# Queries ahead of attention and tokens ahead of keys in a one-core MetaFormer block

## The reference

```
n  = layernorm over channels(x)                        # eps 1e-6
k  = relu(Wk n + bk);  q = relu(Wq n + bq);  v = Wv n + bv     # 1x1 convolutions, 8 heads of 8 channels
context  = k v^T, summed over all 16384 pixels of an image, per head
x1 = x + Wr (context^T q) + br
t  = layernorm over channels(x1)                       # eps 1e-5
p  = softmax(t router_w + router_b)                    # 8 experts; the two largest kept, normalised to sum 1
out = x1 + sum over the two experts of p_e * (t expert_w[e] + expert_b[e])
```

## Time and profile before

| what | value |
|---|---|
| median of 3 runs | 696.85 us (696.65 to 698.34) |
| profiled execution, its own time | 696.26 us |
| its span, first to last instruction | 694.4 us |
| TensorE matmuls busy | 632.0 us (91%) |
| VectorE busy | 531.5 us (77%) |
| ScalarE busy | 422.6 us (61%) |
| GpSimd busy | 396.6 us (57%) |
| mean granted TensorE clock | 0.99 |

### The profile page before, as it was taken

One profiled execution on the slowest core, in us unless ns is written; L12 is line 12 of the kernel. 1 busy time (PEld: TensorE's weight loads), 2 busy tenths in 40 slices (PEclk: granted clock), 3 DMA queues, 4 the chain that ended last, 5 costly groups with the idle time before them and its releaser, 6 DMA issues.

```text
span 694.4 us, 21531 instructions
## 1 busy us (share of the span) xinstructions
PE 632.0 (91%) x8318; PEld 281.6 (41%) x8318; DVE 531.5 (77%) x1176; ACT 422.6 (61%) x832; POOL 396.6 (57%) x350
## 2 busy tenths in 40 slices
PE   3799899799999999999999999999988989896886
PEld 1566655444444444444444444443222223231222
DVE  3443457788788988887888888877999898988854
ACT  2355466767576776767576676767566575664542
POOL 7132432166556656656555665555766566575785
PEclk9999999999999999999999999999999999999999
DMA  6223545755566565555556655444655555463442
GB/s 144 61 66 94 124 123 135 177 135 138 122 154 153 125 151 140 126 133 139 120 141 154 147 129 123 107 119 114 150 123 122 122 123 136 102 149 85 106 107 47
DMA packets 32664, 86.22 MB, mean 124 GB/s; under 512 B 7651, under 2 KB 7827, under 8 KB 32563
## 3 DMA queue, kind: packets, MB, share of 16 engines
q1 hardware_dynamic: 32082, 84.64, 50.9%
q0 software_dynamic: 288, 0.19, 0.1%
q10 hardware_dynamic: 192, 0.01, 0.0%
HBM read 34.47 MB, written 16.78 MB: 74 GB/s over the span
## 4 chain that ended last, share of the span: by engine, by line
PE 62%; DVE 21%; issue 8%; ACT 7%; POOL 1%; DVEq 0%; ACTq 0%; POOLq 0%
PE bank L1077 24%; PE bank L1000 7%; PE bank L1063 7%; PE bank L978 5%; DVE z L812 4%; PE bank L947 4%; DVE x L716 3%; PE bank L1074 3%; DVE osb L822 2%; ACT grows L560 2%; PE bank L1049 2%; PE bank L964 2%; PE bank L923 2%; PE bank L909 2%; PE bank L1024 1%
## 5 line engine op out<-in xcount | busy, mean ns | idle before, releaser
L433 POOL TENSOR_TENSOR z<-gbs,x1d 128x512 f32<-128x512 f32 x256 | 320.8, 1275 | 212.3 <-ACT gbs L566 113.9
L1080 PE MATMUL bank<-z,ew 128*64 128x512 f32 x512 | 247.7, 607 | 0.0
L1077 PE MATMUL bank<-z,ew 128*64 128x512 f32 x512 | 247.6, 607 | 0.0
L812 DVE TENSOR_TENSOR z<-bank,x1d 128x512 f32<-128x512 f32 x256 | 163.2, 679 | 19.6 <-PE bank L1063 19.3
L566 ACT COPY gbs<-bank 128x512 f32<-128x512 f32 x256 | 140.4, 594 | 55.3 <-PE bank L1063 52.3
L1063 PE MATMUL bank<-grows,sel 64*64 64x512 f16 x1024 | 98.3, 391 | 27.9 <-DVE z L812 17.0
L424 POOL TENSOR_TENSOR xsq<-xin 128x512 f32<-128x512 f32 x64 | 65.4, 1044 | 78.3 <-DMA xin<-in_x_dram 74.4
L1077 PEld LDWEIGHTS bank<-z,ew 128*64 128x64 f32 x512 | 65.7, 138 | 105.6 <-issue 95.7
L494 ACT COPY xn<-bank 128x512 f32<-128x512 f32 x64 | 34.4, 589 | 77.0 <-PE bank L923 77.0
L671 DVE TENSOR_TENSOR xnT<-bank,rstd 128x512 f32<-128x512 f32 x64 | 41.2, 685 | 36.8 <-PE bank L909 34.6
L1063 PEld LDWEIGHTS bank<-grows,sel 64*64 64x64 f16 x1024 | 26.9, 104 | 103.4 <-issue 29.8
(11 more groups left out here) (135 smaller groups left out, 823.9 us busy)
## 6 DMA issues: line engine op xcount, KB each, us to landing
x1d<-x SPq DMA_DIRECT2D x128, 256.0 KB, 4.4
xin<-in_x_dram SPq DMA_DIRECT2D x64, 256.0 KB, 4.1
x_again<-in_x_dram SPq DMA_DIRECT2D x64, 256.0 KB, 4.1
out_dram<-osb SPq DMA_DIRECT2D x128, 128.0 KB, 2.4
k<-in_const_dram SPq DMA_DIRECT2D x1, 453.5 KB, 3.8
ew_nat<-in_L_ffn_expert_w_dram POOLq DMA_DIRECT2D x2, 64.0 KB, 6.3
sel<-in_const_sel_dram SPq DMA_DIRECT2D x1, 128.0 KB, 3.4
bk_rows<-bk_wide ACTq DMA_DIRECT2D x6, 1.0 KB, 1.7
```

The lines of the kernel that those rows point to most:

```text
L433: pool.tensor_tensor(z[:, 1, i % R_Z, :], gbs[:, i % R_Z, :], x1d[:, g % 2, 1, u * NT:(u + 1) * NT], ALU.mult).then_inc(z_pool, 1)
L812: dve.tensor_tensor(z[:, 0, i % R_Z, :], bank[:, :], x1d[:, g % 2, 0, u * NT:(u + 1) * NT], ALU.mult).then_inc(taken_of(("spread", i, 0)), 1)
L1077: pe.matmul(out_bank[0:C, :], ew[:, j, :], z[:, 0, i % R_Z, :], start=False, stop=(j == PAIRS - 1), skip_group_check=True).then_inc(prod_d ...
L1080: pe.matmul(out_bank[C:P, :], ew[:, j, :], z[:, 1, i % R_Z, :], start=False, stop=(j == PAIRS - 1), skip_group_check=True).then_inc(prod_d ...
```

## The change

In slot 2 TensorE and ScalarE take the queries first, then the first spread, then attention; before it was attention, first spread, queries. The bank list follows, and the ring of queries gets a ninth slot. In slot 0, from n = 17 on, TensorE transposes tokens first, then makes columns, then keys; ScalarE takes columns before keys. On VectorE `normalise` goes ahead of the gate steps of its slot, and the first z product of slot 2 ahead of the residuals. The work values of the deviation steps move from SBUF (`bstat`) to PSUM bank 7 (`dev_work`, in the columns of `g_all`), and 1 + exp goes to columns of `g_own` (`second_work`), for which `choose` moves behind the reciprocal. The 27 gate steps get other phases, `root_dev` moves from phase 0 to phase 1 (slot 2 of an even step), and the first gate step now waits for `low` of the pair before.

The parts below are, in order: the ring and the banks, ScalarE (slot 0, where TensorE's list changes likewise, and slot 2), the gate steps and slots of VectorE, and slot 2 of TensorE.

```diff
-R_X, R_Q, R_X1, R_Z = 3, 8, 7, 4
+R_X, R_Q, R_X1, R_Z = 3, 9, 7, 4
...
-        bstat = sb("bstat", [P, 5, QG])
-        gstat = sb("gstat", [P, 6, QG])
+        bstat = sb("bstat", [P, 4, QG])
+        gstat = sb("gstat", [P, 5, QG])
...
+        dev_work = [bank[7][:, QG * E + QG * i:QG * E + QG * (i + 1)] for i in range(2)]
+        second_work = bank[7][:, 0:QG]
...
-            gate_steps = {0: root_dev, 5: exponent, 7: high, 8: low}
+            gate_steps = {1: root_dev, 5: exponent, 7: high, 8: low}
...
-                    if k == 0:
+                    if k == 0 and n >= L_EXPERTS:
+                        if has_rows(n - L_COLS):
+                            take_cols(n - L_COLS)
+                        if real(n - L_KEYS):
+                            for s in range(S):
+                                take_keys(n - L_KEYS, s)
+                    elif k == 0:
...
-                        for i in iterations(n, k + 1)[:1]:
-                            copy_gates(i)
                         if real(n - L_KEYS):
                             for s in range(S):
                                 take_queries(n - L_KEYS, s)
+                        for i in iterations(n, k + 1)[:1]:
+                            copy_gates(i)
...
+                    upto(dve, low_done, p * 2)
-                    return dve.scalar_tensor_tensor(halves(bstat[:, 0, :]), mean, -1.0, mean, ALU.mult, ALU.mult)
+                    return dve.scalar_tensor_tensor(halves(dev_work[0]), mean, -1.0, mean, ALU.mult, ALU.mult)
...
-                dev = newton(bstat[:, 3, :], bstat[:, 4, :], bstat[:, 2, :], (bstat[:, 1, :], bstat[:, 0, :]))
+                dev = newton(bstat[:, 0, :], bstat[:, 3, :], bstat[:, 1, :], dev_work)
-                    lambda: dve.tensor_tensor(halves(bstat[:, 1, :]), halves(bstat[:, 0, :]), square, ALU.add),
-                    lambda: dve.tensor_scalar(bstat[:, 2, :], bstat[:, 1, :], 0.0, EPS_FFN, ALU.max, ALU.add),
-                    lambda: dve.reciprocal(bstat[:, 0, :], bstat[:, 2, :]),
+                    lambda: dve.tensor_tensor(halves(dev_work[1]), halves(dev_work[0]), square, ALU.add),
+                    lambda: dve.tensor_scalar(bstat[:, 1, :], dev_work[1], 0.0, EPS_FFN, ALU.max, ALU.add),
+                    lambda: dve.reciprocal(bstat[:, 2, :], bstat[:, 1, :]),
...
+                    lambda: dve.tensor_scalar(second_work, gstat[:, 4, :], 1.0, None, ALU.add),
+                    lambda: dve.reciprocal(gstat[:, 3, :], second_work),
                     choose,
-                    lambda: dve.tensor_scalar(gstat[:, 3, :], gstat[:, 5, :], 1.0, None, ALU.add),
-                    lambda: dve.reciprocal(gstat[:, 4, :], gstat[:, 3, :]),
                     gate,
...
-            gates_by_phase = {8: (26, 27), 0: (0, 4), 2: (4, 9), 3: (9, 12), 4: (12, 16), 6: (16, 20), 7: (20, 26)}
+            gates_by_phase = {8: (26, 27), 1: (0, 4), 2: (4, 10), 3: (10, 12), 4: (12, 14), 5: (14, 16), 6: (16, 23), 7: (23, 26)}
...
+                    if k == 0 and real(n - L_TURN):
+                        for s in range(S):
+                            normalise(n - L_TURN, s)
                     if k == 1:
...
                     if k == 2:
                         if real(n - L_EXPERTS):
                             result(n - L_EXPERTS, 0)
+                        for i in iterations(n, k + 1)[:1]:
+                            product(i)
                         if real(n - L_ATTEND):
...
+                        if real(n - L_KEYS):
+                            make_queries(n - L_KEYS)
+                        for i in iterations(n, k + 1)[:1]:
+                            broadcast(i)
                         if real(n - L_ATTEND):
                             attend(n - L_ATTEND)
-                        for i in iterations(n, k + 1)[:1]:
-                            broadcast(i)
-                        if real(n - L_KEYS):
-                            make_queries(n - L_KEYS)
```

More of the change, by code:

```diff
@@ L74, in bank_uses @@
                 yield "fold", *folding(n, k)
-            if k == 0:
+            if k == 0 and n >= L_EXPERTS:
+                if real(n - L_TURN):
+                    yield from (("turned", n - L_TURN, s) for s in range(S))
+                if has_rows(n - L_COLS):
+                    yield "cols", n - L_COLS, 0
+                if real(n - L_KEYS):
+                    yield from (("keys", n - L_KEYS, s) for s in range(S))
+            elif k == 0:
                 if real(n - L_KEYS):
@@ L87, in bank_uses @@
             if k == 2:
+                if real(n - L_KEYS):
+                    yield from (("queries", n - L_KEYS, s) for s in range(S))
+                for i in iterations(n, k + 1)[:1]:
+                    yield from (("spread", i, s) for s in range(S))
                 if real(n - L_ATTEND):
                     yield from (("attended", n - L_ATTEND, u) for u in range(U))
-                for i in iterations(n, k + 1)[:1]:
-                    yield from (("spread", i, s) for s in range(S))
-                if real(n - L_KEYS):
-                    yield from (("queries", n - L_KEYS, s) for s in range(S))
             if k == 3:
@@ L532, in root_dev @@
                 act.wait_ge(gate_dve, p * N_GATE + 4)
-                nc.scalar.activation(bstat[:, 4, :], bstat[:, 0, :], ACT.Sqrt).then_inc(dev_root, 1)
+                nc.scalar.activation(bstat[:, 3, :], bstat[:, 2, :], ACT.Sqrt).then_inc(dev_root, 1)
             def exponent(p):
@@ L538, in exponent @@
                 nc.scalar.activation(gex[:, :, :], g_own, ACT.Exp).then_inc(exp_done, 1)
-                nc.scalar.activation(gstat[:, 5, :], gstat[:, 2, :], ACT.Exp).then_inc(exp_done, 1)
+                nc.scalar.activation(gstat[:, 4, :], gstat[:, 2, :], ACT.Exp).then_inc(exp_done, 1)
             def high(p):
@@ L724, in gates @@
                 first = first_wins.unsqueeze(1).to_broadcast([P, QG, E])
-                over_dev = over_experts(bstat[:, 3, :])
+                over_dev = over_experts(bstat[:, 0, :])
                 def start():
@@ L736, in choose @@
                 def choose():
-                    dve.wait_ge(exp_done, p * 2 + 2)
                     return dve.tensor_tensor(g_own, g_all, gex[:, :, :], ALU.mult)
                 def gate():
-                    return dve.tensor_tensor(g_all, g_own, over_experts(gstat[:, 4, :]), ALU.mult)
+                    return dve.tensor_tensor(g_all, g_own, over_experts(gstat[:, 3, :]), ALU.mult)
                 def left():
@@ L748, in scale @@
                 def scale():
-                    upto(dve, low_done, p * 2)
                     return dve.tensor_tensor(by_half(g_own),
@@ L766, in less_second @@
                 def less_second():
[L767 removed]
+                    dve.wait_ge(exp_done, p * 2 + 2)
                     return less(g_all, 2)()
[L770 removed]
+                dev = newton(bstat[:, 0, :], bstat[:, 3, :], bstat[:, 1, :], dev_work)
                 steps = [
                     start,
[L773 to L775 removed]
+                    lambda: dve.tensor_tensor(halves(dev_work[1]), halves(dev_work[0]), square, ALU.add),
+                    lambda: dve.tensor_scalar(bstat[:, 1, :], dev_work[1], 0.0, EPS_FFN, ALU.max, ALU.add),
+                    lambda: dve.reciprocal(bstat[:, 2, :], bstat[:, 1, :]),
                     rooted, dev[1], dev[2],
@@ L890, in _ @@
                             gates(quad_in(n, k, phase), k0, k1)
-                    if k == 0 and real(n - L_TURN):
-                        for s in range(S):
-                            normalise(n - L_TURN, s)
-                    for i in iterations(n, k + 1):
+                    for i in iterations(n, k + 1)[1 if k == 2 else 0:]:
                         product(i)
@@ L1109, in _ @@
                         fold(*folding(n, k))
-                    if k == 0:
+                    if k == 0 and n >= L_EXPERTS:
+                        if real(n - L_TURN):
+                            turn_x(n - L_TURN)
+                        if has_rows(n - L_COLS):
+                            to_columns(n - L_COLS)
+                        if real(n - L_KEYS):
+                            make_keys(n - L_KEYS)
+                    elif k == 0:
                         if real(n - L_KEYS):
```

1 line of the change is left out of this document (removed).

## The result

| | before | after |
|---|---|---|
| median of 4 runs each, in turn on one chip | 697.58 us (696.65 to 698.34) | 671.88 us (671.37 to 675.24) |
| ratio | | 0.9632, interval 0.9603 to 0.9660 |
| span of the profiled execution | 694.4 us | 670.1 us |

678 us was predicted, with 664 to 690 as the range.

What follows compares the result with a forecast made beforehand. TensorE bounds the steady part; late, TensorE and VectorE pass stalls to each other. Steady +1.1, late -8.0, -3.9 and -1.3, clock -4.5, n = 16 -2.5 sum to -19.1 us: 678 us, range 664 to 690.

Steps and rivals of the forecast that it cites:

- Late part: Steps from n = 36: moved gate steps remove two stalls, 2.0 us saved per even step 36 to 42, 8.0 in all.
- 1.3 us at slot 3's spread: Late even steps: held L730 and the root ahead of the `grows` copy delay slot 3's spreads, 1.3 us (0 to 1.5).
- 3.9 of some 4.8: Step n = 44: spreads wait 2.16 in one place and 1.4 in slot 0; 3.9 us taken as saved.
- Rival 3: PSUM work does not free VectorE from GpSimd; L773 and L792 stay at 1.15 to 1.19: 689 us, chance 0.1.
- Slot 2: Steady part, queries first: +0.85 us in 8 even steps, -0.6 in 9 odd ones, -0.7 in n = 34.
- Slot 0: Steady part, tokens and columns before keys: -4.8 us for one stall, +5.2 for z products asked for earlier.
- The -4.8 for the stall on the last bank: Slot 0's spreads wait for the bank of `cols`, emptied after both key copies; 0.28 goes in 17 steps.
- the +5.2 for the wait on the next boundary: `cols` and `keys` take z products' banks 1.3 us earlier, behind seven odd-step gate steps: 0.65 us, 8 times.
- The fill: n = 16: normalise goes ahead of its slot's gate steps, so transposes wait less and the clock recovers: 2.5 us saved.
- Rival 1: ScalarE is in time in even steady steps, or its lateness is absorbed: about 659 us, chance 0.1.
- Rival 2: L730 and the root do not hold the late steps, 4 x 1.3 us: 672 us, chance 0.15.
- Rival 4: Slower: pauses of 1.5 us in even steady steps and 1.3 in late ones lower the clock: 700 us, chance 0.06.

Runs made afterwards that it cites:

- e4: e3 with the three gate work arrays left in SBUF instead of PSUM; 691.0 us, ratio 0.9888.
- e3: The change's gate steps alone (new places and PSUM values), with the old order of slots 0 and 2; 671.88 us, ratio 0.9619.
- e10: The full change with the old order of slot 2 (gates' change and slot 0's new order stay); 667.34 us, ratio 0.9559.
- e6: The full change with ScalarE's `low` moved behind the query copies in slot 2; 669.36 us, ratio 0.9605.
- e2: The kernel before with the new order of slot 0 alone, normalise ahead of the gate steps; 705.26 us, ratio 1.0102.
- e7: The full change with normalise put back behind the gate steps for n < 17; 677.79 us, ratio 0.9718.
- e8: The full change with the mean copied to PSUM for L746, one VectorE instruction more; 670.98 us, ratio 0.9625.
- e5: The kernel before with only 1 + exp written to PSUM and `choose` behind the reciprocal; 695.03 us, ratio 0.9958.
- e11: The full change with the mean copied to PSUM and, from n = 18 on, `low` behind the queries; 663.75 us, ratio 0.9510.
- e1: The kernel before with the new order of slot 2 alone and nine query slots; 702.63 us, ratio 1.0063.
- e13: e10 with the mean copied to PSUM (slot 2 old, `low` in its old place); 665.57 us, ratio 0.9534.

## Why the prediction was right or wrong, step by step

**Late part, right in kind, its rest too large.** Both stalls went; L746 stays held (1.10 for the 1.18 I took), the old L773 and L792 are free (0.20), and the clock kept 2.4 GHz from 500 to 640 us. I had put 1.3 us at slot 3's spread and found 0.74, 0.5 at the next result and found 0.19 (at 526.34). So the even step saves 2.97 and not 2.0, four times: 3.9 us of the 5.2 by which the forecast was too high. The stretch behind n = 44 gave 7.5 for 6.6; of the forecast's "3.9 of some 4.8" for n = 44 its rows hold only 2.16 and 1.4, 3.6 in all.

**Rival 3 refuted, by a wide margin.** PSUM does free VectorE: e4 against e3, 19 us. My text had the gain of the placement in the late part alone; it also pays 7.4 us in the steady part, because only it makes the new places there harmless. The step that failed here is a term put at nothing: I had no line for the gates' move in the steady part. By itself it gave 2.9 us (e3, 305.04 against 307.96).

**Slot 2, right in even steps, wrong in odd ones.** Even: +0.85 forecast for each step, 0.75 found against the earlier trace rows, and 0.85 against e10 (3.77 for 2.92). Odd: -0.6 forecast, -0.46 found (2.77 for 3.23), but against e10 only 0.15 (2.77 for 2.92). The step that failed: I took the old order's stall from the rows of before, and the gates' move had already shortened it there. So I had slot 2's order at +0.7 in all; the runs show +6.5 (e10 to the full change), of which 0.85 and -0.15 in eight pairs make 5.6 by an estimate. e6 shows the named cause, `low` ahead of the query copies, directly.

**Slot 0, wrong sign.** The -4.8 for the stall on the last bank holds (0.32 in an odd step for the 0.28 I took). The +5.2 for the wait on the next boundary was the error: the wait for xnT is there, 8 times, but 3.5 us in all, not 5.2, and e10 against e3 gives the whole order as -5.9 where I had +0.4 (both marks of this stretch move alike). Where these come from shows in the spread of slot 0 of an even step, timelines of e3 and then of e10:

```profile
392.08 0.91 PE L1063 MATMUL bank<-grows,sel 64*64 64x512 f16 x8
```

```profile
389.42 0.77 PE L1076 MATMUL bank<-grows,sel 64*64 64x512 f16 x8
```

In the odd step it falls from 0.92 to 0.60, and in both steps the keys pass to the next group 0.93 us after their start instead of 1.03, which I had not counted. Together these are 0.66 of each pair of steps, which fell from 37.98 to 37.33. So beside the new gates little is left of the wait that I feared, 0.17 in an even step. Had the gates stayed where they were, it would have cost 6.4 (e2): what I feared of the old gate steps exists, in the even step and not at the boundary.

Slot 2 and slot 0 erred in opposite directions, 5.8 and -6.3, and these cancel nearly. The steady part came out at -2.3 for +1.1, and 2.9 of that difference is the gates' move, which I had at nothing. The total was right for reasons that held by half.

**The fill, wrong sign.** I took 2.5 us back in n = 16 for normalise going first. Timeline of the changed kernel, n = 16:

```profile
133.00 0.71 PE L938 MATMUL bank<-k,xnT 64*128 64x64 f32 x16 [1.36 <-DVE xnT L686]
...
137.65 1.06 ACT L562 ACTIVATE gT<-bank 128x256 f16<-128x256 f32 x2
...
138.86 0.61 PE L1064 MATMUL bank<-eye,gT 128*128 128x128 f16 x8 [3.27 <-ACT gT L562]
```

The wait for xnT fell from 2.03 to 1.36 as wanted, and then the gates of the first pair, now behind normalise, came late: `low` at 137.65 and a pause of 3.27 at their transpose, which before was 0.70. I counted what the step moved ahead gains and left out who waits for the steps that it is moved past. That the gates wait because normalise stands ahead is borne out by the kernels with that order (3.27 in e10 as well) and by e7 without it (0.43). But the larger loss is one step earlier: n = 15 takes 10.47 us where it took 8.65. Timeline of the changed kernel, n = 15:

```profile
117.24 0.94 DVE L652 SCALAR_TENSOR_TENSOR xstat<-xstat 128x16 f32<-128x16 f32 x1
...
118.22 0.97 DVE L653 TENSOR_TENSOR xstat<-xstat 128x16 f32<-128x16 f32 x1
...
122.70 0.70 PE L938 MATMUL bank<-k,xnT 64*128 64x64 f32 x16 [1.53 <-DVE xnT L686]
```

Two small steps of the statistics of x, from SBUF to SBUF, met GpSimd's squares of x (117.12 to 119.16) and took 0.94 and 0.97 us for 0.17. Six gate steps stand between them and normalise, and TensorE waited 1.53 us for it. It is the same hold as in the late part, at a place that I had not priced. In e10 the two took 0.11 and 0.17 and the step 8.72, so it depends on what happens to run beside them.

The clock was the other part of that term; no drop stands in n = 16 in the changed kernel, but there is one in the windows from 75 to 95 us that the kernel before has not, whose cause is open.

**Other rivals.** Rival 1 (ScalarE in time) is refuted by the 23.3 us of waits for q (its 659 also left out the +1.1 of the forecast that it replaces; by its own terms it is 657.6); e6 is that rival made true, and takes the steady pair to 37.3 (298.69 / 8), below the 37.5 that the forecast named as its sign. Rival 2 (no hold of the late steps) is half true: 0.74 for 1.3. Rival 4 (slower by the clock) did not come about: with pauses of 0.74 and less at one place, no late step lost its clock.

## What to carry to other kernels

Price a reordering against the kernel that has all other parts of the change, not against the kernel before: two orders were worth +4.4 and +7 us alone, and +4.5 and -4.5 beside the third. When small VectorE values lie beside GpSimd work, look at least and most of one line's durations: 190 to 1180 ns for the same 32 columns are a wait inside the instruction, and the cheap cure is PSUM: for one of two SBUF inputs, or for the output of a step with one. Whoever moves a step ahead must list who waits for the steps that it passes, in the fill as well. Whoever moves small VectorE steps must list what GpSimd does beside their new places and beside all that they push back.

## What the runs showed of the hardware

**Which operand counts.** With a GpSimd product beside it, a VectorE instruction of 32 columns with two SBUF inputs and a PSUM output is held (L746: up to 1177 ns), one with one SBUF and one PSUM input never (L787, L749: 198 to 200 in 16 of 16; twelve of e3's L774 and eight of e8's L749 lie wholly within a GpSimd TENSOR_TENSOR). But a TENSOR_SCALAR with one SBUF input and an SBUF output is held as well (L791 in e4: 1094 in the median, 1153 at most; L792 in the earlier trace rows is the same), and not with its output in PSUM (L804 and e5: 195 in all). A reader who takes one SBUF input as always safe misses this. The Trainium skill (SBUF — State Buffer, Who interferes with whom) has both halves: a VectorE instruction with two SBUF inputs contends with a GpSimd instruction that reads SBUF, and copies, casts and tensor_scalar can run in a mode that takes the shared ports too. L746 agrees with the first, e4 and e5 with the second. RECIPROCAL from SBUF to SBUF took 352 to 355 ns in all 32 instructions of the kernel before and all 32 of e4, where 15 of the 16 of L792 lie wholly within a GpSimd TENSOR_TENSOR.

**The clock.** The late even steps of e5 have 0.95 us less of VectorE work than before and a clock of 0.90 in each; the changed kernel and e11 had a like gap at n = 16, and only e11 lost its clock behind it. Over the executions of the kernel before in the groups of e1 to e13 the mean granted clock went from 0.977 to 0.993, so one execution's clock is not read as a property of an edit. The stretches between marks at full clock agree between kernels to 0.1 us (107.54, 107.52, 107.51), and small differences were read from them and not from the medians.
